# Layer 2's experts with slots folded by VectorE and packed table words; scores and shares in another order

## The reference, cut to what matters

```python
leaf = 0
for d in range(4):
    logits = xf @ Wr[off:off + cnt].T + br[off:off + cnt]     # off = 2**d - 1, cnt = 2**d
    leaf = leaf * 2 + (logits[n, leaf] > 0)
out[n] = gelu(xf[n] @ W1[leaf] + b1[leaf]) @ W2[leaf] + b2[leaf]   # 512 -> 2048 -> 512
```

## Time and profile before

| | |
|---|---|
| median of 3 runs | 1865.62 us (1865.12 to 1866.37) |
| profiled execution | 1858.58 us |
| its span | 1856.8 us, 26229 instructions |
| busy: PE, PEld, DVE, ACT, POOL | 90%, 55%, 43%, 25%, 7% |
| mean granted TensorE clock | 0.94 |
| read from HBM | 226.93 MB, 127 GB/s over the span |
| layer 1's experts | from about 634 us |
| layer 2's attention | from about 863 us |
| layer 2's routing, expert loop, tail | about 1243, 1281 to 1592, to 1622 us |

### The profile page before, as it was taken

One profiled execution on the slowest core, in us unless ns is written; L12 is line 12 of the kernel. 1 busy time (PEld: TensorE's weight loads), 2 busy tenths in 40 slices (PEclk: granted clock), 3 DMA queues, 4 the chain that ended last, 5 costly groups with the idle time before them and its releaser, 6 DMA issues. The chain is left out here.

```text
span 1856.8 us, 26229 instructions
## 1 busy us (share of the span) xinstructions
PE 1662.3 (90%) x8818; PEld 1017.1 (55%) x8819; DVE 805.0 (43%) x2087; ACT 473.2 (25%) x930; POOL 124.0 (7%) x188
## 2 busy tenths in 40 slices
PE   6889889999999799988999999988888988699973
PEld 3345564576456498985677656654333323265532
DVE  6665376821366664535534346341111111412555
ACT  2012224420010222222654136201222321231220
POOL 0011000000000003440000000000000000110000
PEclk9798999999999899997999989989999999799996
DMA  5131136100251359952000201047997584140000
GB/s 155 62 116 34 53 104 230 55 6 1 79 222 35 120 211 266 273 168 66 23 22 2 102 31 50 0 185 307 408 397 334 236 342 185 42 143 1 1 1 28
DMA packets 68812, 236.44 MB, mean 127 GB/s; under 512 B 13453, under 2 KB 17156, under 8 KB 61825
## 3 DMA queue, kind: packets, MB, share of 16 engines
q1 hardware_dynamic: 54187, 207.37, 30.2%
q0 software_dynamic: 14544, 28.01, 5.1%
HBM read 226.93 MB, written 8.39 MB: 127 GB/s over the span
## 5 line engine op out<-in xcount | busy, mean ns | idle before, releaser
L101 PE MATMUL psum<-ahead_arena 125*125 125x257 f32 (+2 forms) x720 | 218.6, 461 | 4.5 <-DVE ahead_W L2461 3.4
L101 PEld LDWEIGHTS psum<-ahead_arena 125*125 125x125 f32 (+1 forms) x720 | 131.3, 189 | 82.2 <-issue 66.3
L715 DVE TENSOR_SCALAR a0e_ring<-a0e_node,a0e_key 125x625 f16 x198 | 70.6, 391 | 69.5 <-PE psum L520 63.4
L101 PE MATMUL psum<-a_W,1_xn_turned 128*125 128x512 f32 x200 | 91.0, 605 | 1.2 <-DVE a_u L1346 1.2
L518 PE MATMUL psum<-a0e_ring,a0e_tables 125*128 x198 | 73.8, 432 | 18.7 <-DVE a0e_ring L715 11.9
L101 PE MATMUL psum<-a_W,a0l_H 128*125 128x512 f32 x190 | 81.9, 592 | 0.7 <-issue 0.7
L2818 PE MATMUL psum<-ahead_arena,ahead_W 128*32 128x256 f32 x928 | 77.6, 385 | 1.9 <-DMA ahead_arena<-in_L_ffn_W 1.9
L2798 PE MATMUL psum<-ahead_arena,ahead_W 128*32 128x256 f32 x928 | 58.5, 393 | 23.1 <-DVE ahead_W L3079 23.1
L101 PE MATMUL psum<-e_xgT,e_W 128*128 128x156 f32 x512 | 73.8, 308 | 3.0 <-issue 3.0
L101 PEld LDWEIGHTS psum<-e_xgT,e_W 128*128 128x128 f32 x512 | 72.4, 200 | 3.8 <-issue 3.8
L3084 DVE COPY ahead_W<-psum 32x512 f32<-32x512 f32 x29 | 19.7, 679 | 120.8 <-PE psum L2805 120.8
(11 more groups left out here) (667 smaller groups left out, 2866.8 us busy)
## 6 DMA issues: line engine op xcount, KB each, us to landing
ahead_arena<-in_L_ffn_W SPq DMA_DIRECT2D x52, 2048.0 KB, 10.3
e_W<-in_L_ffn_W SPq DMA_DIRECT2D x16, 2048.0 KB, 11.7
1_xn_turned<-half_shares SPq DMA_DIRECT2D x16, 256.0 KB, 9.0
a_stage<-in_L_gnn_W SPq DMA_DIRECT2D x8, 512.0 KB, 7.5
ahead_arena<-in_L_gnn_W SPq DMA_DIRECT2D x2, 2048.0 KB, 10.3
a_W<-in_L_gnn_W SPq DMA_DIRECT2D x3, 1024.0 KB, 5.1
a_qkv<-half_shares SPq DMA_DIRECT2D x11, 256.0 KB, 3.2
a_W<-in_L_ffn_w_down POOLq DMA_DIRECT2D x1, 2816.0 KB, 16.4
```

Source lines behind the costliest of these rows:

```text
L101: last = nc.tensor.matmul(bank[0:rows, at:at + cols], lhs, rhs, start=(n == 0), stop=(n == len(terms) - 1))
L715: nc.vector.tensor_scalar(ring[:, bass.ds(at, 1), 0:NODES].rearrange("p a n -> p (a n)"), node[:, :], key[:, k, bass.ds(t, 1)], None, ALU. ...
```

## The change

1. *Fold*: the product is gone. VectorE adds three of the four partial sums of PSUM to the first, which is in `part`, the last addition into `y`.
2. *Table*: six rows; first slot, count and heavy count share a word, as do first token and expert. Each engine loads one or two words a visit and takes the fields out by shift and mask.
3. *Last slot*: it isn't folded or stored. `part` is spread to the nodes' rows by five products with a matrix that marks, for every node in the last slot, its four partial sums. For that, TensorE spreads all places ahead of the loop. Zeros are stored at its place.
4. *Bias rows*: GpSimd fetches each node's row of `b2` by five indirect DMAs ahead of the loop. The turning of `oh` and the bias products are gone.
5. *Routing*: a 512-wide product into `sums` stands ahead of the small ones; one wait covers four results; `fold`'s constants are replaced by lane numbers.
6. *Layer 1*: shares are spread before any edges are turned, and the two tables are copied behind the shares.
7. *Layer 2's scores* are made in layer 2, between the first and second projection, from which `sources` follows.

The diff, cut to its core:

```diff
 # layer1_ffn, TensorE (ScalarE's keeps are moved alike)
-                for t in range(2):
-                    masks(t)
                 pe.wait_ge(sem["shares_known"], 1)
                 spread(0)
                 spread(1)
-                for t in range(2, TILES):
+                for t in range(TILES):
                     masks(t)
...
+                for t in range(TILES):
+                    next_rows(t)
 # layer1_ffn, VectorE
-                dve.wait_ge(sem["place_made"], 1)
-                step(nc.vector.tensor_copy(place[:, :], place_i))
-                nc.vector.tensor_copy(numbers[:, :, :], numbers_i[:, :, :])
                 dve.wait_ge(sem["exponents_done"], 1)
...
                 dve.wait_ge(sem["shares_known"], 1)
+                dve.wait_ge(sem["place_made"], 1)
+                step(nc.vector.tensor_copy(place[:, :], place_i))
+                nc.vector.tensor_copy(numbers[:, :, :], numbers_i[:, :, :])
 # layer2_attention, TensorE (ScalarE alike)
                 project(0, 0, 0)
+                scores(0)
+                project(0, 0, 1)
                 sources(0, 0)
-                for t in range(1, 4):
+                for t in range(2, 4):
                     project(0, 0, t)
 # layer2_ffn: fields of the table
+            def slots_at(eng, q):
+                v = word(eng, 1, q, 2 ** 19 - 1)
+                return within(v >> 12, 0, 2 * MOST), within((v >> 6) & 63, 1, MOST), within(v & 63, 1, MOST)
+            def tokens_and_expert(eng, q):
+                v = word(eng, 3, q, 2 ** 14 - 1)
+                return within(v >> 4, 0, NODES + SL - 1), within(v & 15, 0, EXP2 - 1)
 # TensorE, routing
+                    nc.tensor.matmul(sums[:, :], c.ident[0:ROWS, :], c.xn[:, 0, :], start=True, stop=True)
                     pe.wait_ge(sem["sizes_made"], 1)
 # TensorE, slot
-                        pe.wait_ge(sem["parts_kept"], s + 1)
-                        pe.wait_ge(sem["y_ready"], s + 1)
-                        nc.tensor.matmul(folds[0:SL, :], fold, part, start=True,
-                                         stop=True).then_inc(sem["folded"], 1)
...
                         pe.wait_ge(sem["upper_gelu"], s + 1)
+                        pe.wait_ge(sem["y_ready"], s + 2)
 # TensorE, ahead of the loop
+                    pe.wait_ge(sem["places_known"], 1)
+                    for t in range(TILES):
+                        bank, at = (order, t * ROWS) if t < 4 else (small, 0)
+                        nc.tensor.matmul(bank[:, at:at + ROWS], posf[:, t:t + 1].to_broadcast([ROWS, 128]),
+                                         c.ident[0:ROWS, 0:ROWS], start=True, stop=True)
+                    pe.wait_ge(sem["final_known"], 1)
+                    nc.tensor.matmul(small[:, 256:257], final[:, :].to_broadcast([1, 128]), ...)
 # TensorE, tail (the turning of oh and the products with b2 are gone)
+                    pe.wait_ge(sem["last_marked"], 1)
                     pe.wait_ge(sem["parts_kept"], slots + 1)
+                    for t in range(TILES):
+                        nc.tensor.matmul(last_rows[t][0:ROWS, :], at_last[:, rows_of(t)], part, start=True,
+                                         stop=True).then_inc(sem["rows_spread"], 1)
 # VectorE, table
+                    step(nc.vector.scalar_tensor_tensor(out=packed[:, 1, :], in0=tab[:, 3, :], scalar=64.0,
+                                                        in1=tab[:, 2, :], op0=ALU.mult, op1=ALU.add))
+                    ...
+                    nc.vector.tensor_copy(tab_i[:, :, :], packed[:, :, :]).then_inc(sem["table_made"], 1)
 # VectorE, slot
-                        dve.wait_ge(sem["folded"], s + 1)
+                        dve.wait_ge(sem["parts_kept"], s + 1)
+                        nc.vector.tensor_tensor(part[0:SL, :], part[0:SL, :], sums[SL:2 * SL, :], ALU.add).then_inc(
+                            sem["two_added"], 1)
+                        dve.wait_ge(sem["two_added"], s + 1)
+                        nc.vector.tensor_tensor(part[0:SL, :], part[0:SL, :], sums[2 * SL:3 * SL, :], ALU.add).then_inc(
+                            sem["three_added"], 1)
+                        dve.wait_ge(sem["three_added"], s + 1)
                         dve.wait_ge(sem["y_free"], s + 1)
-                        nc.vector.tensor_copy(y, folds[0:SL, :]).then_inc(sem["y_ready"], 1)
+                        nc.vector.tensor_tensor(y, part[0:SL, :], sums[3 * SL:4 * SL, :], ALU.add).then_inc(
+                            sem["y_ready"], 1)
 # VectorE, tail
+                    nc.vector.tensor_scalar(at_last[:, 0:4 * ROWS], order[:, 0:4 * ROWS], lane[:, 0:1], None, ALU.is_equal)
+                    ...
+                    nc.vector.memset(y, 0.0).then_inc(sem["y_ready"], 1)
+                    dve.wait_ge(sem["bias_fetched"], TILES * 16)
+                    for t in range(TILES):
+                        nc.vector.tensor_tensor(c.x[:, t, :], c.x[:, t, :], c.xn[:, t, :], ALU.add)...
+                    for t in range(TILES):
+                        dve.wait_ge(sem["rows_spread"], t + 1)
+                        nc.vector.tensor_tensor(c.x[:, t, :], c.x[:, t, :], last_rows[t][0:ROWS, :], ALU.add)...
 # GpSimd, ahead of the loop
+                    gp.wait_ge(sem["final_known"], 2)
+                    gp.wait_ge(sem["sorted_freed"], 2 * CH)
+                    for t in range(TILES):
+                        nc.gpsimd.indirect_dma_start(
+                            out=c.xn[:, t, :], out_offset=None, in_=d["L2_ffn_b2"],
+                            in_offset=bass.IndirectOffsetOnAxis(ap=own[:, t:t + 1], axis=0)).then_inc(
+                                sem["bias_fetched"], 16)
```

More of the change, by code:

```diff
@@ L1879, in _ @@
                 norm.on_vector(dve, 0, last)
-                take("scores")
+                dve.wait_ge(sem["scalar_freed"], for_scalar.nth(("next", TILES - 1)))
             @block.sync
@@ L2768, in _ @@
                     nc.tensor.matmul(small[0:1, 260:266], c.ones[0:EXP2, 0:1], V[:, :], start=True,
-                                     stop=True).then_inc(sem["before_ready"], 1)
-                    nc.tensor.matmul(folds[0:ROWS, 0:EXP2], heavy[:, 0:1].to_broadcast([EXP2, ROWS]),
-                                     c.ident[0:EXP2, 0:EXP2], start=True, stop=True).then_inc(sem["heavy_spread"], 1)
+                                     stop=True)
+                    nc.tensor.matmul(wide[0:ROWS, 0:EXP2], heavy[:, 0:1].to_broadcast([EXP2, ROWS]),
+                                     c.ident[0:EXP2, 0:EXP2], start=True, stop=True).then_inc(sem["spread"], 1)
                     for n in range(2 * CH):
@@ L2848, in _ @@
                     both, visits = visits_of(pe)
+                    pe.wait_ge(sem["places_known"], 1)
[4 more added lines that the diff above has]
+                    pe.wait_ge(sem["final_known"], 1)
+                    nc.tensor.matmul(small[:, 256:257], final[:, :].to_broadcast([1, 128]), c.ones[0:1, 0:1], start=True,
+                                     stop=True).then_inc(sem["spread"], 1)
                     pe.wait_ge(sem["sorted_freed"], 2 * CH)
-                    pe.wait_ge(sem["constants_made"], 1 + QT)
+                    pe.wait_ge(sem["constants_made"], 1)
                     with pe.Fori(0, both) as i:
-                        first, count, more = field(pe, 3, i), field(pe, 2, i), field(pe, 6, i)
+                        first, count, more = slots_at(pe, i)
                         with pe.Fori(0, count) as j:
@@ L2878, in _ @@
                         for s in range(TILES):
-                            last = nc.tensor.transpose(hid[s // 4][0:ROWS, s % 4 * 128:s % 4 * 128 + ROWS],
-                                                       c.AT[:, s, rows_of(t)], c.ident[0:ROWS, 0:ROWS])
+                            bank, at = (order, s * 128) if s < 4 else (small, 0)
+                            last = nc.tensor.transpose(bank[0:ROWS, at:at + ROWS], c.AT[:, s, rows_of(t)],
+                                                       c.ident[0:ROWS, 0:ROWS])
                         last.then_inc(sem["edges_turned"], 1)
-                        if t >= 2:
-                            pe.wait_ge(sem["bias_added"], t - 1)
-                        nc.tensor.matmul(core.bank(6 + t % 2)[0:ROWS, :], ohT[:, rows_of(t)], b2, start=True,
-                                         stop=True).then_inc(sem["bias_ready"], 1)
                 @block.scalar
@@ L3164, in _ @@
                     with gp.Fori(0, both) as i:
-                        first, count, more = field(gp, 3, i), field(gp, 2, i), field(gp, 6, i)
-                        start = field(gp, 1, i)
+                        first, count, more = slots_at(gp, i)
+                        start = tokens_at(gp, i)
                         with gp.Fori(0, count) as j:
@@ L3171, in _ @@
                     with gp.Fori(both, visits) as i:
-                        first, count = field(gp, 3, i), field(gp, 2, i)
```

(3 more changed lines are left out.)

157 lines of the change are left out of this document (88 added, 69 removed).

## The result

| | before | after |
|---|---|---|
| median of 12 runs each, us | 1864.7 | 1854.7 |
| lowest and highest, us | 1861.6, 1874.6 | 1849.3, 1861.0 |
| ratio after / before, with its 95% interval | | 0.9943 (0.9925 to 0.9961) |
| profiled execution: time, span, us | 1858.6, 1856.8 | 1854.9, 1853.2 |

The change gains 10 us of the 32 that I forecast, and the time lies 6 us outside my range. The two spans differ by only 3.6 us, because the unchanged code ahead of layer 1's experts took 6.6 us longer in the profiled execution after and the unchanged end 4.7 less. So I cut both spans at the same instructions.

The account below looks back on a forecast made before the run. In layer 2's experts, TensorE's order of work and 8.39 MB of weights per visit were taken as close limits. Loop 20.6 + tail 7.9 + shares 4.0 + scores 0 = 32.5 us gained, forecast 1833.1 us, range 1821 to 1849.

Parts of the forecast that it names:

- the one at the loop's entry: Layer 2's experts, entry: bias gathers take 3.9 us before the second visit's weights; 2.1 us gained (-1 to 4).
- rival (b): Layer 2's expert loop: the store of `y` becomes each slot's cycle; about 1869 us at a 9.5 us landing; chance 0.05.
- The fold: Expert slots: 9.48 becomes 8.62 us; VectorE's additions of 0.69 fit; the third waits for the previous slot's stored `y`.
- Packed words: Borders between visits: fewer table loads cut the border from 2.0 to 1.0 us, a gain of 1.0 each.
- What the DMA makes of it: Two-slot visits: weights and stores limit them to 19.6 us, so five periods gain 1.37 each, 6.9 together.
- The loop as a whole: Layer 2's expert loop: entry, slots and borders less waits for weights sum to a gain of 20.6 us.
- The wait behind the single slot's visit: Layer 2's loop: the next visit's loads start only once the single slot's weights have landed, costing 2.0 us.
- Tail: Last copy of partial sums to layer 3: final gathers go out earlier, gaining 7.9 us (bounds 5 and 10).
- shares: Layer 1: shares no longer need GpSimd's numbers or two tiles of turned edges; 4.0 us gained (0 to 6).
- scores: Scores moved into layer 2: earlier start offset by their cost there and by VectorE/GpSimd overlap; sum 0 (-2 to +3).
- Rival (a): Layer 2's loop: weights hide more, visits stay at 20.97 us; gain 21.5, time 1844 us; chance 0.22.
- (d): Layer 2's loop: VectorE's additions take longer, slots stay at 9.48, only the tail pays; 1853 to 1866 us; chance 0.05.

Follow-up runs that it names:

- late: Changed kernel with its five gathers of bias rows moved behind the first store of the last visit: 1833.9 us, ratio 0.9831.
- none: Changed kernel without the five gathers of bias rows, five VectorE operations of the same length kept in their place: 1834.3 us, ratio 0.9857.
- foldp: Changed kernel with gathers moved to the last visit, and a slot's fold again by TensorE's product and a VectorE copy: 1839.7 us, ratio 0.9881.
- words: Changed kernel with gathers moved to the last visit, and every table field again read by its own load: 1840.7 us, ratio 0.9876.
- direct: Changed kernel with five plain loads of 125 rows of 2048 bytes in place of the five gathers: 1839.4 us, ratio 0.9864.
- w4k: Changed kernel, gathers in their old place, each 2 MB weight load issued as four quarter-column loads (4 KB packets): 1857.9 us, ratio 0.9957.

## Why the prediction was wrong

*The step that failed* is the one at the loop's entry, "Behind them, in the same DMA engines, come the five gathers of bias rows": it prices them as bytes, 3.9 us of full rate in front of the second visit's weights, and asks nothing of what stands behind them. Two things were wrong in it. The gathers did not go ahead of the weights but beside them, in turns, and were through at 1329 rather than within 4 us. And the stores of `y` are issued by GpSimd too, behind the gathers, with VectorE's next addition behind each store. I had the chain in hand: the fold's own step says that the third addition waits for the stored `y`, and rival (b) is this mechanism. I set it aside because "6.9 is the longest of 29", from a trace in which nothing else was on GpSimd's queue; that row could not speak for a kernel that puts five gathers there. It decided in one slot, not in every slot, so it came to 26 us and not to (b)'s price. Shown by: gathers moved, no stall; one gather, none; plain loads with 25 packets, 6.6 us; weights in quarter packets, 0.8.

The Trainium skill, "DMA: Bandwidth & Descriptors", section "Queues, rings and completion order", has the rule that I did not weigh: each DMA engine goes round the queues that have work and serves a packet of each in turn. The trace agrees from 1302 to 1311 (257 to 258), and nearly so from 1290 to 1314 (556 to 580); from 1287 to 1290 it does not (44 to 306). The same section gives such a packet 9 to 17 descriptors; no run here shows how many descriptors one of the profile's packets holds.

*The fold.* Right: slots of 8.76 (forecast 8.62), additions of 0.68, 0.68 and 0.69, and the next VectorE operation not held up.

*Packed words.* Right in kind, too small: the border went from 2.0 to 0.6, forecast 1.0.

*What the DMA makes of it.* Right: 19.8 to 19.9 per two-slot visit in `late`, `none`, `foldp` and `words`, forecast 19.6. What I had not seen is that either part alone reaches this limit: with packed words TensorE needs 2 x 9.49 + 0.9 = 19.9, with the fold alone 2 x 8.76 + 2.2 = 19.7. The 5.3 us of the five periods are paid for twice.

*The loop as a whole:* 330.1 - 310.6 = 19.5 in `late`, forecast 21.5. The sum is close because errors cancel. From the heavy expert's first load to the second visit's first slot `late` gained 6.0 us, forecast 3.0, since the 3.9 us of gathers are not there. The five periods gave 5.3 for 6.9, as visits took 19.9 us and not 19.6. From the seventh visit's first slot on it was 8.2 for 11.7: 3.3 of that is the slot of 12.2 us beside the gathers. The wait behind the single slot's visit came as forecast, 17.2 to 19.3 (forecast 19.2), but reached 22.0 in `none`.

*Tail* 7.5 (forecast 7.9), *shares* 4.2 (4.0), *scores* -0.3 (0), heavy expert's load 1.1 later (0.9): right within the bounds given. `late`, the changed kernel without the stall, took 1833.9 us; the forecast was 1833.1. That they agree within 1 us is partly luck, by the sum just told: against its own runs of the kernel before, `late` gains 30.6 of the 32.5. Rival (a) is out (visits are not at 21), and so is (d).

## What to carry to other kernels

Before adding a transfer, list what the same engine issues behind it and who waits for that landing; a landing time read while the queue was otherwise empty says nothing of it. Price a gather beside a bulk load by its packets on each engine and the other queue's packet time, not by its bytes alone, and take the product as a lower bound: it gave 41.5 us where 41.5 were measured, but 15 for 25.1 in `direct` and 10.9 for 19.7 in `w4k`. Or put the gather where no bulk load runs. And where two limits lie within 5% of each other, two edits that each reach the second limit are worth one of them there.

## What the hardware showed that I had not expected

- Two queues on the same DMA engines took turns by packets and not by bytes: from 1302 to 1311, 258 packets with 10 KB in all against 257 with 3.69 MB. From 1287 to 1290 they did not (306 to 44).
- While data packets of both queues alternated, the total fell, too: from 1290 to 1302 to 324 GB/s, and a packet of SyncE's queue took 0.864 x 16 x 12 / 225 = 0.74 us in the mean, instead of 0.984 x 16 x 9 / 257 = 0.55 from 1302 to 1311. The queues of the changed kernel in those 12 us:

```profile
DMA packets 474, 3.89 MB, mean 324 GB/s; under 512 B 145, under 2 KB 145, under 8 KB 264
...
q1 hardware_dynamic: 225, 3.41, 86.4%
q0 software_dynamic: 247, 0.46, 14.9%
```

- The same unchanged code of 634 us took up to 10 us more or less from one execution to the next, with the places where TensorE's granted clock falls.
